# A graph network's aggregations on one core: gathering aligned chunks of edges and walking a list of (chunk, tile) pairs

## The chip, the cores and the metric

The kernel runs on one core of a Trainium2 chip. The metric is the device time of one execution in microseconds (us), from the first to the last instruction of that core; the number that counts is the median over several runs.

## What is computed

A graph has N = 6250 nodes with 256 features each (fp32) and E = 100000 edges `src -> dst`, sorted by `dst`. Four residual blocks follow one another. Each normalizes the node rows, and each contains one sum over the edges:

```
h = relu(layernorm(x));  x = x + block0(h): segment_sum(table0[src], dst), then experts
h = relu(layernorm(x));  x = x + block1(h): segment_sum(table1[src], dst)
h = relu(layernorm(x));  x = x + block2(h): segment_sum(table2[src], dst)
h = relu(layernorm(x));  x = x + block3(h): segment_sum(tensor_product(table3[src], edge weights), dst)
```

The edge weights of block 3 come from a small two-layer network on 8 numbers of every edge. The draw of `dst` is uneven: it is 6250 u² for a uniform u.

## The kernel before

**Tiles and windows.** The nodes lie in T = 50 tiles of P = 125 rows. `prepare` counts the edges of each tile and cuts each tile's edges into windows of 128 (`WIN`); a window belongs to one tile, so the last window of a tile is filled up with edges of the next one, which match no row of it. There are room and instructions for `WINDOWS` = 832 windows. The table `win_tab` holds each window's tile and first edge. Windows behind the last tile begin at edge E, where the padded edge list has `src` 0 and `dst` -1. `load_windows` gathers the windows' edges (8 indirect transfers of 104 windows) and turns them, so that `src_w[:, w]` and `dst_w[:, w]` are the 128 sources and local destinations of window w, in SBUF.

**One aggregation** (`aggregate`, run as agg0, agg1 and agg2 for blocks 0 to 2) makes 52 iterations of `WPI` = 16 windows, all written out:

- GpSimd (POOL) gathers the 128 rows of a window from the table in HBM into one of 16 buffers `msg` (L713), when VectorE has staged their indices (L726), which it does for four windows at a time once their buffers are free.
- VectorE (DVE) makes a one-hot matrix by comparing a row of numbers with `dst_w` (the match, L733), six windows ahead.
- TensorE (PE) multiplies one-hot and messages into one of four PSUM banks (L826, two passes of fp32), as soon as the gather has landed.
- VectorE adds the bank to the row block of the window's tile (L745; in agg0 also the in-degrees, L744). The tile comes out of a register: 16 of them are loaded at a time (`load_values`, L117).

Beside that, the same loop runs the edge network of block 3, in batches of 384 edges, two an iteration (262 batches: 104, 104 and 54): PE's L802 and L809, ScalarE's (ACT) L845, L854 and L855, and SyncE's (SP) loads of inputs (L887, L888) and stores of results (L893). agg0 and agg1 also do a product of the node's own rows in each iteration up to the 50th (L832, L834). In agg2 the one-hot matrices are stored (L898) for `tensor_product_edges`, the stage of block 3, which walks the same 832 windows and reads `src_w`.

**Counting.** In `prepare`, VectorE compares all destinations (125 x 800) with the upper bound of each of the 50 tiles, with a sum over the row (L375); PE adds over partitions, and a chain of small VectorE steps (`Chain`: each waits for the one before) makes the tables. After that VectorE makes the one-hot matrices of a histogram of `src` until the end of the stage.

Of the kernel before, what the change touches and what calls it, by code (L numbers as in the profile page):

```python
# [32 lines left out]
ds = bass.ds  # L33
# [10 lines left out]
STEPS = WINDOWS // WPI  # L44
BATCH = 3
# [14 lines left out]
assert N == P * T and E == P * EC and T % 2 == 0 and WINDOWS == WG * GROUPS_W and WG <= Q  # L60
assert EPAD >= E + WIN and 4 * STEPS < BATCHES <= 6 * STEPS and BATCHES % 2 == 0

# [52 lines left out]
def load_values(eng, row, most):  # L115

    return eng.bass.values_load_multi_w_load_instructions(  # L117
        row, engines=[eng.engine], min_val=0, max_val=most,
        skip_runtime_bounds_check_because="the table of windows is clamped to these bounds where it is written")[1]
# [24 lines left out]
class Net:  # L144


    def __init__(self, nc, ctx, a):
# [8 lines left out]
        self.src_w = sb("src_w", [Q, WINDOWS], I32)  # L156
        self.dst_w = sb("dst_w", [Q, WINDOWS])
        self.win_tab = sb("win_tab", [1, 2 * WINDOWS], I32)
# [104 lines left out]
def prepare(net, outb):  # L263
# [3 lines left out]
    with net.phase("prep") as ph:  # L267
# [7 lines left out]
        SCRATCH = 16  # L275
        scratch = [base[:, (9 + k) * EC:(10 + k) * EC] for k in range(SCRATCH)]
        tiles_bf, lanes_bf = ph.sb("tiles_bf", [P, EC], BF16), ph.sb("lanes_bf", [P, EC], BF16)
# [13 lines left out]
        past = ph.sb("past", [T, WINDOWS])  # L291
# [3 lines left out]
        iota_w = ph.sb("iota_w", [T, WINDOWS])  # L295
# [9 lines left out]
        with ph.block() as block:  # L305
            @block.gpsimd
            def _(pool):
# [10 lines left out]
                pool.wait_ge(s_const, 5)  # L318
# [33 lines left out]
            def _(act):  # L352
                act.wait_ge(s_ids[1], 96)
                for to, of, rows in ((net.edges, a["edge_index"], 192), (net.attr, a["edge_attr"], 192)):
# [3 lines left out]
                              a["edge_scal_t"].rearrange("k (r n) -> (k r) n", r=32)).then_inc(s_copies, 16)  # L358
                act.wait_ge(s_copies, 48)

            @block.vector
            def _(dve):
                step = Chain(dve, s_step)
                dve.memset(zero_bf[:, :], 0.0).then_inc(s_zero, 1)
                dve.wait_ge(s_const, 7)
                dve.tensor_copy(iota_bf[:, :], net.iota_i[0:P, 0:P])
                step(dve.tensor_scalar(bounds[:, :], net.iota_i[0:P, 0:T], float(P), float(P), ALU.mult, ALU.add))
# [3 lines left out]
                step(dve.tensor_copy(dst_f, ids[1]))  # L371
# [5 lines left out]
                dve.wait_ge(s_below, T)  # L377
                dve.tensor_copy(count[:, 0:1], below[:, 0:1])
                dve.tensor_tensor(count[:, 1:T], below[:, 1:T], below[:, 0:T - 1], ALU.subtract)
# [3 lines left out]
                dve.wait_ge(s_cnt, 2)  # L383
# [8 lines left out]
                dve.tensor_scalar(past[:, :], iota_w[:, :], col[:, 4:5], None, ALU.is_ge).then_inc(s_past, 1)  # L392
                dve.wait_ge(s_sum, 4 + 2 * GROUPS_W)
                for k in (0, 1):
# [11 lines left out]
                                  ALU.min, ALU.mult)  # L406
                dve.wait_ge(s_b2, 16)
                split_parts(Chain(dve, s_b2_split), dve, [part[:, :] for part in b2_parts], b2[:, :])

                dve.wait_ge(s_ids[0], 32)  # L410
# [16 lines left out]
            def _(pe):  # L427
                pe.wait_ge(s_const, 7)
                pe.wait_ge(s_below, T + 1)
                pe.matmul(small[0:T, 0:1], count[:, :], net.ones[0:P, 0:1], start=True, stop=True).then_inc(s_cnt, 1)  # L430
                pe.matmul(small[0:1, 2:3], bad[:, :], net.ones[0:P, 0:1], start=True, stop=True).then_inc(s_cnt, 1)
                pe.wait_ge(s_pairs, 1)
# [6 lines left out]
                for g in range(GROUPS_W):  # L439
# [3 lines left out]
                              start=True, stop=True).then_inc(s_sum, 1)  # L443
                pe.wait_ge(s_zero, 2)
# [137 lines left out]
def load_windows(net):  # L582

    with net.phase("windows") as ph:
        got = [ph.sb(f"got{g}", [WG, 2 * WIN], I32) for g in range(GROUPS_W)]
        src = [ph.sb(f"src{g}", [WG, WIN]) for g in range(GROUPS_W)]
        dst = [ph.sb(f"dst{g}", [WG, WIN]) for g in range(GROUPS_W)]
        s_got, s_flat, s_turned = ph.sem("got"), ph.sem("flat"), ph.sem("turned")
        of_src, of_dst = net.bank[0:2], net.bank[2:4]
        with ph.block() as block:  # L590
            @block.gpsimd
            def _(pool):

                for g in range(GROUPS_W):
                    pool.indirect_dma_start(
                        out=got[g][:, :], out_offset=None, in_=net.edges[:, :],
                        in_offset=bass.IndirectOffsetOnAxis(ap=net.first_edge[:, g:g + 1], axis=0)).then_inc(s_got, 16)

            @block.vector
            def _(dve):  # L600
                dve.wait_ge(s_got, 16 * GROUPS_W)
                for g in range(GROUPS_W):
                    dve.tensor_copy(src[g][:, :], got[g][:, 0::2]).then_inc(s_flat, 1)
                    dve.tensor_scalar(dst[g][:, :], got[g][:, 1::2], net.base_col[:, g:g + 1], None,
                                      ALU.subtract).then_inc(s_flat, 1)
                dve.wait_ge(s_turned, 2 * GROUPS_W)
                half = WINDOWS // 2
                for k in (0, 1):
                    dve.tensor_copy(net.src_w[:, k * half:(k + 1) * half], of_src[k][:, 0:half])
                    dve.tensor_copy(net.dst_w[:, k * half:(k + 1) * half], of_dst[k][:, 0:half])  # L610

            @block.tensor
            def _(pe):
                for g in range(GROUPS_W):
                    pe.wait_ge(s_flat, 2 * g + 2)
                    k, c = divmod(g, GROUPS_W // 2)
                    for of, to in ((src[g], of_src[k]), (dst[g], of_dst[k])):
                        pe.transpose(to[:, WG * c:WG * (c + 1)], of[:, :], net.ident[0:WG, 0:WG]).then_inc(s_turned, 1)
# [18 lines left out]
def aggregate(net, tag, table, degrees=False, root=None, shift=None, batches=(0, 0), kept_hots=None):  # L637
# [6 lines left out]
    GROUPS = 4  # L644
    PER = WPI // GROUPS
    AHEAD = 12
    HOTS, HOT_AHEAD = 8 if kept_hots is None else 16, 6
    KEPT = HOTS // BLOCK
    BANKS = 4
    with net.phase(tag) as ph:  # L650
        msg = [ph.sb(f"msg{r}", [Q, sums]) for r in range(WPI)]
        if kept_hots is None:
            hots = [ph.sb(f"hots{r}", [Q, BLOCK, HOT_W]) for r in range(KEPT)]
        else:
            size = BLOCK * HOT_W
            hots = [net.acc_full[:, T * D + r * size:T * D + (r + 1) * size].rearrange("p (b n) -> p b n", n=HOT_W)
                    for r in range(KEPT)]
        hot = [hots[r // BLOCK][:, r % BLOCK, :] for r in range(HOTS)]
        s_stored = [ph.sem(f"stored{r}") for r in range(KEPT)]
        idx = [ph.sb(f"idx{g}", [Q, PER], I32) for g in range(GROUPS)]  # L660
        s_idx, s_idle = ph.sem("idx"), ph.sem("idle")
        s_msg = [ph.sem(f"msg{r}") for r in range(WPI)]
# [31 lines left out]
        with ph.block() as block:  # L694
            @block.gpsimd
            def _(pool):
# [6 lines left out]
                if degrees:  # L703
                    for r in range(WPI):
                        pool.memset(msg[r][:, D:sums], 1.0).then_inc(s_ones, 1)

                def body(i, tile, last):
                    for g in range(GROUPS):
# [3 lines left out]
                        for r in range(PER):  # L712
                            pool.indirect_dma_start(  # L713
                                out=msg[PER * g + r][:, 0:D], out_offset=None, in_=table[:, :],
# [1264 lines left out]
```

## Time and profile before

| | us |
|---|---|
| median of 3 runs | 5958.91 (5951.58 to 5963.21) |
| the profiled execution, its own time | 5952.01 |
| its span (first to last instruction) | 5950.3 |

| engine | busy us (share) |
|---|---|
| PE matmul | 4674.6 (79%) |
| PE weight load | 3416.2 (57%) |
| DVE | 3725.1 (63%) |
| ACT | 1922.8 (32%) |
| POOL | 3687.2 (62%) |

The shares are means over stages that have different limits, so the views below are cut by stage. PE is TensorE's matmul, PEld its weight load, a "q" behind an engine's name its sequencer (register, semaphore and DMA-issuing work, not counted as busy). A row of the timeline is start, length, engine, line, operation, output <- inputs, count, and in brackets the idle time of the engine before it with what ended it. A row of the groups by line has busy time and mean ns of one, then idle time before it and what ended most of it. PEclk is the granted clock of TensorE as a share of full speed. A row of busy time by stage is the stretch (from:to), its length, the busy us (and count of instructions) of PE, PEld, DVE, ACT and POOL, then PEclk, the mean busy share of the DMA engines and GB/s.

### The profile page before, as it was taken

How to read it: one execution, taken by the hardware profiler on the slowest of the kernel's cores; microseconds unless marked ns; L12 is line 12 of the kernel's file. 1: busy time of each engine (PE TensorE's matmuls, PEld its weight loads, DVE VectorE, ACT ScalarE, POOL GpSimd, SP SyncE). 2: the span in 40 equal slices, each digit the busy share in tenths (PEclk: the TensorE clock that was granted, in tenths of full speed). 3: DMA queues.
4: the chain of work that ended last, by engine and by line, in shares of the span. 5: the costliest groups of instructions: out<-in, count | busy, mean ns of one | idle time of the engine just before them, and what ended most of it. 6: DMA issues, size and time to landing. Idle time of an engine off the chain costs nothing. (4 is left out here: it accounts for less than half of the span.)

```text
span 5950.3 us, 95247 instructions
## 1 busy us (share of the span) xinstructions
PE 4674.6 (79%) x22329; PEld 3416.2 (57%) x22329; DVE 3725.1 (63%) x11556; ACT 1922.8 (32%) x6042; POOL 3687.2 (62%) x4020
## 2 busy tenths in 40 slices
PE   3577777777499996777777767666777699999997
PEld 2554444445289995544444444433333588888887
DVE  8746666665812116655555554555555599999996
ACT  0142222222022222422222233221000577777774
POOL 0157777772066662477777746777777367777771
PEclk9999999996699998999999988999667699999998
DMA  6045555555099996455555556666555388888884
GB/s 176 16 130 148 147 146 148 148 148 98 1 338 338 339 336 171 117 148 146 147 148 148 148 98 176 198 199 195 157 157 157 71 248 260 259 261 259 259 260 99
DMA packets 694298, 1062.47 MB, mean 179 GB/s; under 512 B 212573, under 2 KB 534187, under 8 KB 693106
## 3 DMA queue, kind: packets, MB, share of 16 engines
q0 software_dynamic: 180864, 480.03, 30.6%
q1 hardware_dynamic: 512819, 571.84, 30.4%
q10 hardware_dynamic: 160, 5.63, 0.3%
q8 instruction: 151, 2.47, 0.2%
q14 instruction: 304, 2.49, 0.1%
HBM read 826.26 MB, written 236.47 MB: 179 GB/s over the span
## 5 line engine op out<-in xcount | busy, mean ns | idle before, releaser
L713 POOL DMA_INDIRECT agg_msg<-table,agg_idx x2496 | 2362.8, 947 | 760.3 <-issue 671.9
L745 DVE TENSOR_TENSOR acc<-acc,bank 125x256 f32 x2496 | 1051.3, 421 | 999.3 <-PE bank L826 948.0
L826 PE MATMUL bank<-agg_msg,agg_hots 128*125 128x257 f32 (+1 forms) x3328 | 1086.8, 421 | 530.0 <-DMA agg_msg<-table,agg_idx 337.0
L826 PEld LDWEIGHTS bank<-agg_msg,agg_hots 128*125 128x125 f32 x3328 | 545.6, 194 | 1061.5 <-DVE agg_hots L733 607.7
L1700 POOL DMA_INDIRECT tp_src<-table,tp_idx x832 | 807.0, 970 | 286.6 <-issue 252.4
L1714 ACT ACTIVATE tp_hots<-tp_hot,tp_weight 128x125 f32<-128x125 f32 x2496 | 814.2, 390 | 277.5 <-PE bank L1731 240.2
L826 PE MATMUL bank<-agg_msg,acc 128*125 128x256 f32 x1664 | 657.2, 502 | 291.5 <-DMA agg_msg<-table,agg_idx 209.8
L1731 PEld LDWEIGHTS bank<-tp_msg,tp_hots 128*125 128x125 f32 x4992 | 679.3, 189 | 47.4
L1731 PE MATMUL bank<-tp_msg,tp_hots 128*125 128x128 f32 x4992 | 684.1, 273 | 0.0
L826 PEld LDWEIGHTS bank<-agg_msg,acc 128*125 128x125 f32 x1664 | 312.8, 228 | 637.2 <-DVE acc L733 413.1
L854 ACT ACTIVATE agg_made<-bank,agg_made 128x128 f32<-128x128 f32 x786 | 288.6, 367 | 1174.2 <-PE bank L809 1162.3
L1727 PE MATMUL bank<-tp_msg,tp_hot 128*125 128x256 f32 x1664 | 557.9, 417 | 31.0 <-DVE tp_msg L1752 29.5
L1765 DVE TENSOR_TENSOR acc<-acc,bank 125x512 f32 x832 | 562.9, 677 | 2.3 <-issue 1.3
L733 DVE TENSOR_SCALAR agg_hots<-iota_i,dst_w 128x126 f32<-128x126 f32 x1664 | 503.9, 304 | 0.0
L809 PE MATMUL bank<-agg_fc,agg_hid 128*128 128x256 f32 x1572 | 486.7, 392 | 0.0
L1752 DVE TENSOR_TENSOR tp_msg<-tp_weight,tp_src 128x384 f32<-128x384 f32 x832 | 455.8, 548 | 0.0
L845 ACT ACTIVATE agg_hid<-bank 128x384 f32<-128x384 f32 x262 | 128.4, 490 | 805.9 <-PE bank L802 805.9
L1561 DVE COPY ffn_res<-bank 128x256 f32<-128x256 f32 x162 | 68.8, 425 | 503.9 <-DMA expert_rows<-ffn_res,moe_row_of_place 449.4
L744 DVE TENSOR_TENSOR deg_in<-deg_in,bank 125x1 f32 x832 | 129.5, 156 | 400.2 <-PE bank L826 380.6
L1474 POOL DMA_INDIRECT ffn_rows<-tokens,moe_token_of x162 | 158.0, 976 | 294.4 <-DVE ffn_b L1547 149.1
L809 PEld LDWEIGHTS bank<-agg_fc,agg_hid 128*128 128x128 f32 x1572 | 312.1, 199 | 48.8
L1537 ACT ACTIVATE ffn_hid<-bank,ffn_b 128x128 f32<-128x128 f32 x648 | 184.6, 368 | 440.4 <-PE bank L1513 440.4
(301 smaller groups left out, 6155.7 us busy)
## 6 DMA issues: line engine op xcount, KB each, us to landing
tp_weight<-edge_rows SPq DMA_DIRECT2D x832, 130.0 KB
edge_rows<-agg_made SPq DMA_DIRECT2D x262, 390.0 KB, 3.6
acc<-in_L_w_laid_dram SPq DMA_DIRECT2D x162, 512.0 KB
acc<-in_L_gnn_w_dram SPq DMA_DIRECT2D x162, 512.0 KB
kept_hots<-acc SPq DMA_DIRECT2D x208, 252.0 KB, 2.5
tp_hot<-kept_hots SPq DMA_DIRECT2D x208, 252.0 KB, 3.9
agg_msg<-table,agg_idx POOLq DMA_INDIRECT x2496, 3.0
table<-tab_out SPq DMA_DIRECT2D x40, 560.0 KB
```

The source lines that it names most:

```text
L713: pool.indirect_dma_start(out=msg[PER * g + r][:, 0:D], out_offset=None, in_=table[:, :], in_offset=bass.IndirectOffsetOnAxis(ap=idx[g][:, ...
L733: dve.tensor_scalar(hot[r % HOTS], net.iota_i[:, 0:HOT_W], net.dst_w[:, ds(WPI * i + r, 1)], None, ALU.is_equal).then_inc(s_hot, 1)
L745: dve.tensor_tensor(row, row, bank[0:P, 0:D], ALU.add).then_inc(s_add, 1)
L809: pe.matmul(wb[n % 2][:, 0:4 * MUL], hid[j % 2][:, c * Q:(c + 1) * Q], fc2[:, :, :].rearrange("p b n -> p (b n)"), start=True, stop=True). ...
L826: pe.matmul(net.bank[w % BANKS][0:P, 0:sums], hot[w % HOTS][:, 0:P], msg[w][:, :], start=True, stop=True).then_inc(s_sum, 1)
L854: act.activation(to[:, :, 0, :], of[:, :, 0, :], ACT.Copy, scale=made[j % 2][:, c, 4 * MUL:4 * MUL + 1])
L1700: pool.indirect_dma_start(out=src[w % R][:, :], out_offset=None, in_=table[:, :], in_offset=bass.IndirectOffsetOnAxis(ap=idx[w // WPI % 2] ...
L1714: ins = act.activation(hots[w % RM][:, c, :], hot[w // BLOCK % RB][:, w % BLOCK, 0:P], ACT.Copy, scale=weight[w % RW][:, 4 * MUL + 1 + c:4 ...
L1727: pe.matmul(out[:, 0:4, :], hot[w // BLOCK % RB][:, w % BLOCK, 0:P], m[:, 0:4, :], start=True, stop=False, skip_group_check=True)
L1731: mm = pe.matmul(out[:, 4 + c:8:3 - c, :], hots[w % RM][:, c, :], m[:, 4:6 + c:1 + c, :], start=False, stop=(c == 2), skip_group_check=True)
L1752: dve.tensor_tensor(quad, bc(wv[:, 2:4, :], 2, [Q, 2, 3, MUL]), bc(sv[:, 1:4, :], 1, [Q, 2, 3, MUL]), ALU.mult).then_inc(s_msg, 1)
L1765: dve.tensor_tensor(row, row, banks[w % len(banks)][0:P, :], ALU.add).then_inc(s_add, 1)
```

## The change

Aggregations no longer gather windows. The edge list is cut into 782 chunks of 128 consecutive edges whatever their tile, and each chunk is gathered once. A list of (chunk, tile) pairs, at most 782 + 49 = 831 and padded to 832, says which tile's rows a chunk is added to; PE, the match and the add make one step a pair. Which buffer of the ring of 16 a pair reads, and how many chunks must have landed, PE takes from registers, loaded 16 at a time from two new tables. SP waits for each gather in turn and counts it into one semaphore; it also waits until the pairs of four chunks are done (a third table) and tells POOL that four buffers are free. ACT now issues the loads and stores that SP issued. agg2 makes a second match a step, for the windows that block 3 still walks. `prepare` makes the pair list beside the window tables, and of the 50 counts 26 stay on VectorE while ScalarE makes 24 as sums of signs. `load_windows` gathers pairs and windows (16 transfers), loads the chunks with one, and stores `src_w` and `dst_w` to HBM; agg2 and `load_node_attr` load them back. The core of the diff:

```diff
+CHUNKS = -(-E // WIN)
+PAIRS = WINDOWS
+RING_C = 16
+PER_C = 4
```

In `prepare` (`BY_SIGN` is 26), on ScalarE and then on VectorE:

```diff
+                for b in range(BY_SIGN, T):
...
+                    act.activation(sign_scratch[n % SIGNS], dst_f, ACT.Sign, bias=middles[:, b:b + 1], scale=-1.0,
+                                   accum_out=signs[:, b:b + 1]).then_inc(s_sign, 1)
...
-                for b in range(T):
+                for b in range(BY_SIGN):
...
+                ceil_div(step, dve, tops[:, :], ends[:, :], WIN, twice_i[:, :], twice[:, :])
...
+                dve.tensor_scalar(past[:, :], iota_w[0:T, :], col[:, 5:6], None, ALU.is_ge).then_inc(s_pair_past, 1)
                 dve.wait_ge(s_b2, 16)
                 split_parts(Chain(dve, s_b2_split), dve, [part[:, :] for part in b2_parts], b2[:, :])
 
+                dve.wait_ge(s_pair_sum, 5 + 2 * GROUPS_W)
...
+                    dve.tensor_scalar(net.tile_of_pair[:, of], tile_h[k][TILE_ROW:TILE_ROW + 1, 0:HALF], float(T - 1), None,
+                                      ALU.min)
...
+                dve.tensor_scalar(net.landed_of_pair, chunk_row, 1.0, None, ALU.add)
```

In `load_windows`:

```diff
+                        out=got_p[g][:, :], out_offset=None, in_=net.edges[:, :],
...
+                        out=got_w[g][:, :], out_offset=None, in_=net.edges[:, :],
...
+                sp.dma_start(net.src_w[:, :], all_src[:, :]).then_inc(s_kept, 16)
+                sp.wait_ge(s_all, 4)
+                sp.dma_start(net.dst_w[:, :], all_dst[:, :]).then_inc(s_kept, 16)
```

In `aggregate`, first on POOL, then on DVE and PE:

```diff
-                        pool.wait_ge(s_idx, GROUPS * i + g + 1)
...
+                for c in range(CHUNKS):
+                    if c % PER_C == 0 and c >= RING_C:
+                        pool.wait_ge(s_free, (c - RING_C) // PER_C + 1)
                         carry_wait(pool, s_idle)
...
+                        in_offset=bass.IndirectOffsetOnAxis(ap=net.src_c[:, c:c + 1], axis=0),
+                    ).then_inc(s_msg[c % RING_C], 16)
...
-                        dve.tensor_copy(idx[r // PER][:, :].bitcast(F32),
...
+                            match(ahead)
+                            if kept_hots is not None:
+                                match_window(ahead)
...
+                    landed = load_values(pe, net.landed_of_pair[:, of], CHUNKS, least=1)
+                    slots = load_values(pe, net.slot_of_pair[:, of], RING_C - 1)
...
-                        pe.wait_ge(s_msg[w], 16 * i + 16)
-                        pe.matmul(net.bank[w % BANKS][0:P, 0:sums], hot[w % HOTS][:, 0:P], msg[w][:, :],
+                        pe.wait_ge(s_landed, landed[w] & COUNT_BITS)
+                        pe.matmul(net.bank[w % BANKS][0:P, 0:sums], hot[w % HOTS][:, 0:P], node_row(msg, slots[w]),
```

There on ACT, then on SP:

```diff
+                        if 1 <= j < count - 1:
+                            load(j + 1)
...
+                            store(j)
...
+                for c in range(CHUNKS):
+                    sp.wait_ge(s_msg[c % RING_C], 16 * (c // RING_C) + 16)
+                    sp.sem_inc(s_landed, 1)
+                    g = (c + 10) // PER_C
+                    if (c + 10) % PER_C == 0 and RING_C // PER_C <= g < GROUPS_C:
...
+                        sp.wait_ge(s_sum, gates[k % WPI] & COUNT_BITS)
+                        sp.sem_inc(s_free, 1)
```

In `load_node_attr`:

```diff
+                sp.dma_start(src_w[:, :], net.src_w[:, :]).then_inc(s_src, 16)
```

## Rows read from the trace of the kernel before

**Rows 1.** Busy time by stage: agg0, agg1, agg2, each with its tail.

```profile
349.60:1418.70 1069.10, 797.24 (x2796) 499.11 (x2796) 656.88 (x2698) 236.53 (x778) 787.44 (x832) 0.95 0.55 144
2453.80:3521.30 1067.50, 794.80 (x2796) 491.08 (x2796) 557.30 (x1915) 217.41 (x728) 786.91 (x832) 0.96 0.55 144
3601.50:4660.30 1058.80, 760.09 (x2100) 400.12 (x2100) 559.50 (x1916) 112.85 (x378) 788.34 (x832) 0.82 0.61 176
```

**Rows 2.** Groups by line, whole span: the gathers, two forms of ScalarE.

```profile
L713 POOL DMA_INDIRECT agg_msg<-table,agg_idx x2496 | 2362.8, 947 | 760.3 <-issue 671.9 <-DVE agg_idx L726 88.4
...
L1784 ACT ACTIVATE tab_rows<-x_res,nmr,rstd 125x256 f32<-125x256 f32 x150 | 90.4, 608 | 27.5 <-DVE nmr L1094 27.5
...
L1595 ACT ACTIVATE acc<-acc 125x256 f32<-125x256 f32 x50 | 17.6, 417 | 55.1 <-DVE acc L1627 55.1
```

**Rows 3.** Line L713, the gathers: length ns min/median/max, and landing.

```profile
L713 POOL DMA_INDIRECT agg_msg<-table,agg_idx x2496: 942/946/1013, 349.6 to 4642.1; - x192
...
DMA to landing us min/median/max: 2.6/3.0/15.9
```

**Rows 4.** Timeline at the end of agg0: the last gather, a late load.

```profile
1389.25 0.95 POOL L713 DMA_INDIRECT agg_msg<-table,agg_idx  x1 [0.30 <-issue]
...
1406.78 1.65 PE L802 MATMUL bank<-agg_scal,agg_fc 128*128 128x384 f32 x2 [10.49 <-DMA agg_made<-attr]
```

**Rows 5.** Timeline in agg2 while work is queued up on PE and DVE.

```profile
3612.51 0.42 DVE L745 TENSOR_TENSOR acc<-acc,bank 125x256 f32 x1
...
3612.84 0.28 DVE L733 TENSOR_SCALAR acc<-iota_i,dst_w 128x126 f32<-128x126 f32 x1
...
3613.14 0.42 DVE L745 TENSOR_TENSOR acc<-acc,bank 125x256 f32 x1
...
3614.37 1.27 PEld L826 LDWEIGHTS bank<-agg_msg,acc 128*125 128x125 f32 x6
...
3615.88 0.81 PE L802 MATMUL bank<-agg_scal,agg_fc 128*128 128x384 f32 x2
...
3616.53 0.38 PE L826 MATMUL bank<-agg_msg,acc 128*125 128x256 f32 x1
```

**Rows 6.** Instructions that read the window table: loads of 16 registers, ns.

```profile
L117 DVEq TENSOR_LOAD <-win_tab x208: 1095/1216/2349, 354.6 to 5830.0; - x104
L117 SPq TENSOR_LOAD <-win_tab x52: 967/977/1217, 4773.0 to 5811.7; - x52
```

**Rows 7.** Line L98, loop bookkeeping elsewhere: register work of TensorE's sequencer, ns.

```profile
L98 PEldq FUSED_REGOPS  x71: 44/44/50, 1428.2 to 5939.5; - x71
L98 PEldq ALU_OP  x71: 32/32/32, 1430.7 to 5941.6; - x71
```

**Rows 8.** Timeline of DVE in the counting and the tables.

```profile
8.75 1.05 DVE L375 TENSOR_SCALAR_CACHE_REDUCE acc<-acc,prep_bounds 125x800 f32<-125x800 f32 x1
...
9.72 1.04 DVE L375 TENSOR_SCALAR_CACHE_REDUCE acc<-acc,prep_bounds 125x800 f32<-125x800 f32 x1
...
60.98 0.15 DVE L235 TENSOR_SCALAR prep_col<-prep_col 50x1 f32<-50x1 f32 x1
61.16 0.15 DVE L236 TENSOR_TENSOR prep_col<-prep_col 50x1 f32<-50x1 f32 x1
...
74.17 0.58 DVE L396 TENSOR_SCALAR win_tab<-bank 1x416 int32<-1x416 f32 x1 [11.42 <-PE bank L442]
...
76.28 0.58 DVE L401 TENSOR_SCALAR win_tab<-acc 1x832 int32<-1x832 f32 x1
...
77.12 0.28 DVE L243 CAST prep_b_part<-prep_b 64x256 bf16<-64x256 f32 x1
...
78.97 0.58 DVE L250 CAST acc<-acc 125x800 f32<-125x800 int32 x1
```

**Rows 9.** Timeline of POOL in the window loads: the last of 8 gathers.

```profile
261.90 0.98 POOL L595 DMA_INDIRECT windows_got<-edges,first_edge  x1 [0.30 <-issue]
```

**Rows 10.** DMA issues: operation, KB each, median us from issue to landing.

```profile
edge_rows<-agg_made SPq DMA_DIRECT2D x262, 390.0 KB, 3.6
```

More of the change, by code:

```diff
@@ L406, in _ @@
                                   ALU.min, ALU.mult)
+                dve.tensor_copy(ends[:, 0:1], small[0:T, 3:4]).then_inc(s_pair, 1)
+                dve.tensor_scalar(some[:, :], col[:, 0:1], 0.0, None, ALU.is_gt).then_inc(s_pair, 1)
+                dve.wait_ge(s_pair, 2)
+                step(dve.tensor_tensor(ends[:, 1:2], ends[:, 0:1], col[:, 0:1], ALU.subtract))
+                ceil_div(step, dve, tops[:, :], ends[:, :], WIN, twice_i[:, :], twice[:, :])
+                step(dve.scalar_tensor_tensor(twice[:, :], tops[:, :], float(WIN), ends[:, :], ALU.mult, ALU.is_gt))
@@ L643, in aggregate @@
     acc = net.acc_view(D)
[L644 to L648, printed above, removed]
+    HOTS, HOT_AHEAD = 8, 6
+    KEPT = 4
     BANKS = 4
     with net.phase(tag) as ph:
[L651 to L662, printed above, removed]
+        msg = ph.sb("msg", [Q, RING_C, sums])
+        hot = [ph.sb(f"hot{r}", [Q, HOT_W]) for r in range(HOTS)]
+        if kept_hots is not None:
+            free, size = net.acc_full[:, T * D:2 * T * D], BLOCK * HOT_W
+            window_hots = [free[:, r * size:(r + 1) * size].rearrange("p (b n) -> p b n", n=HOT_W) for r in range(KEPT)]
+            dst_w = free[:, KEPT * size:KEPT * size + WINDOWS]
+            s_stored, s_dst, s_window = [ph.sem(f"stored{r}") for r in range(KEPT)], ph.sem("dst"), ph.sem("window")
+        s_idle, s_landed, s_free = ph.sem("idle"), ph.sem("landed"), ph.sem("free")
+        s_msg = [ph.sem(f"msg{r}") for r in range(RING_C)]
         s_hot, s_sum, s_add = ph.sem("hot"), ph.sem("sum"), ph.sem("add")
@@ L765, in body @@
                             dve.tensor_tensor(row, row, side[0:P, 0:D], ALU.add)
-                for r in range(0, AHEAD, PER):
-                    stage(0, r)
-                for r in range(HOT_AHEAD):
-                    match(0, r)
+                if kept_hots is not None:
+                    dve.wait_ge(s_dst, 16)
+                for p in range(HOT_AHEAD):
+                    match(p)
+                    if kept_hots is not None:
+                        match_window(p)
                 dve.sem_inc(s_add, BANKS)
@@ L865, in body @@
                             act.activation(node_root(net, i), side[0:P, 0:D], ACT.Copy).then_inc(s_rooted, 1)
+                act.wait_ge(s_empty, 5 if root or shift else 4)
+                load(0)
+                load(1)
                 iterations(act, body)
+                for b in (0, 1):
+                    act.wait_ge(s_kept[b], 16 * (count // 2))
+                if kept_hots is not None:
+                    for r in range(KEPT):
+                        act.wait_ge(s_stored[r], 16 * (WINDOWS // BLOCK // KEPT))
             @block.sync
```

313 lines of the change are left out of this document (208 added, 105 removed).

## Prediction

> **What bounds the kernel now.** I read the busy time by stage first. The three aggregations take 1069.1, 1067.5 and 1058.8 us [rows 1], together 3195.4, over half the span. PE, DVE and POOL all show idle time in them, so the shares don't name the limit. The second view, the groups by line, does: the 2496 gathers have 2362.8 us of work and 760.3 us of gaps in front of them, that is 3123.1 / 2496 = 1.251 us from one to the next, and 671.9 us of the gaps were ended by nothing but POOL's own issuing [rows 2]. The gap that is put down to VectorE's staged indices is no wait either: 0.30 us stands ahead of a gather with or without one. A gather's own length hardly varies, 942 to 1013 ns [rows 3]. So POOL issues gathers back to back, and 831 steps of 1.251 us are 1039.7 us of each stage: **the number of gathers sets the stage**, while PE and DVE follow.
>
> What is left of each stage is a tail behind the last gather: 1069.1 - 1039.7 = 29.4 us, then 27.8 and 19.1. A normal gather lands 3.0 us after its issue, the slowest after 15.9 [rows 3], and at the end of agg0 a small load of the edge network was also 10 us late [rows 4]. The place fits the padding. Counting the drawn `dst` by tiles of 125 nodes gives 808 windows with edges; the last 24 gathers fetch table row 0 on all 128 lanes. I read the tail as 24 gathers, and whatever shares the queues with them, crowding on one row.
>
> **The change part by part.** The sum starts from the profiled execution, 5952.0 us (span 5950.3); the median of the runs is 6.9 us above it, so 7 us of the answer are open by that alone.
>
> *Fewer gathers.* 782 chunks instead of 832 windows: 50 x 1.251 = 62.6 us a stage, **-187.7** for three. POOL's instructions stay the same (a wait and an increment ahead of every four). Four buffers come free when SP has seen the pairs of a group done; it looks when a chunk 10 ahead of POOL's next group has landed, so PE may lag 13 gathers (16 us) before POOL waits; a landing takes 3.0.
>
> *The tail.* Only the last chunk is padded, on 96 lanes. I expect landing 3, the crowded chunk 2, matmul and add 1, the last batch's copies and store 1 + 0.4 + 3.6 [rows 10], and 1 to leave: 12 us in agg0 and agg1, and 9 in agg2, which has no batch there. That is 17.4 + 15.8 + 10.1, **-43.3**. From below nothing of it comes (the tail has another cause); from above 51, if a tail is 8 us.
>
> *Does PE follow?* The list has 831 real pairs (same count of the inputs), so PE must do 832 steps in 977 us: 1.175 us a step, and 1.11 at the end, where tiles have 8 chunks and 9 pairs. Where work is queued, a pass of 256 columns takes 1.27 / 6 = 0.212 us and L802's two take 0.65 [rows 5]. Sixteen steps need 32 x 0.212 = 6.8, two batches 2 x (0.65 + 6 x 0.212) = 3.8, the node's own rows 6 x 0.212 = 1.3: 11.9, or 0.74 a step. New are two register loads in 16 steps. None is seen on PE; VectorE's take 1.22 (1.10 to 2.35), SP's 0.98 [rows 6]: 0.12 to 0.29 a step, I take 0.15. The address and the count to wait for are register work, 44 + 44 + 32 ns if it is like the loop bookkeeping [rows 7]: 0.12, or nothing where the sequencer runs ahead. Together 1.01, between 0.86 and 1.15: below 1.175, at its worst just over 1.11. Cost **0**. The cover is POOL's pitch; every 0.01 us above it would cost 8 us a stage. SP's relay of a landing is a wait and an increment, delay but no pitch.
>
> *Does DVE follow?* One add and one match take 3613.14 - 3612.51 = 0.63 us [rows 5]. agg2's second match makes it 0.91, and a register load in 16 steps 0.99 (1.06 if no two instructions overlap). That fits below 1.11. The staging copies (L726) go. Gathers average 5 ns above their minimum beside one match each [rows 2, 3]; a second match costs another 5 x 782, **+4**. agg2's first matches now wait for `dst_w`, about 5 us; POOL can issue 16 gathers (20 us) first, so it is hidden.
>
> *ACT's transfers.* ACT now waits for a batch's store (3.6 us [rows 10]) before it loads the next but has 8 steps, 9 us, for that and 2.5 us of own work; the load has some 3 steps left to land. **0**; if it is late, PE's in-order queue stalls at L802, and the ring of 16 takes up to 16 us of it.
>
> *Counts and tables.* 24 comparisons of 0.97 us leave VectorE [rows 8]: -23.3. ScalarE does 24 beside its 26 (25.2 us, and 2 for the order test). One of 800 columns is not seen: 256 columns take 0.42 to 0.61 [rows 2], so 1.30 to 1.90 in proportion and less by their fixed share. I take 1.1, 26.4 and a table load, just hidden: +0.5; at 1.90 it is +20. The pair list repeats the window list on the same path: 19 chained steps of 0.18 = 3.4, a hop to PE and a comparison 1.3, PE's second set of products 11.4 (the wait in front of L396), four half rows at 0.5, eight whole rows at some 0.75 (a half row's 0.58 is the bound below, twice it above), 0.9 of small ones; the splitting from L243 to L250, 1.85, now runs inside that wait. Together 3.4 + 1.3 + 11.4 + 2 + 6 + 0.9 - 1.85 = 23.2. Net **+1**, between -8 and +22.
>
> *Loading windows.* Eight more gathers at 0.98 + 0.30 [rows 9] are 10.3, and behind them the store of the two tables, like the 390 KB store 3.6 + 0.4 [rows 10]. All of it is alone on the path: **+14.3** (10 to 20). Reading one back in `load_node_attr`: **+1.5** (0 to 4).
>
> Sum: 5952.0 - 187.7 - 43.3 + 4 + 1 + 14.3 + 1.5 = **5742**.
>
> **A rule against it.** The gathers keep their length of 942 to 1013 ns although a match runs beside most of them [rows 3], and that row is what I go by. The Trainium skill (SBUF — State Buffer, Who interferes with whom) says that a VectorE `tensor_scalar` in its two-port mode locks GpSimd out of their shared ports for the whole instruction, and that descriptors can't be written meanwhile. By that rule 832 more matches stall agg2's gathers; that is the rival "locked gathers" below.
>
> **The rivals.**
> *PE becomes the bound* (the one on the other side). Place: the register loads and waits ahead of each pair in PE's queue. For it: nothing in this trace shows PE loading registers or waiting for a register's value. Against it: 1.01 of 1.175. At 1.20 us a step each stage takes 832 x 1.20 + 14 = 1012 instead of 989: 5811. It decides when three stages take what they did less the 17 us added elsewhere, (3195.4 - 17) / 3 = 1059, (1059 - 14) / 832 = 1.256 us a step; above that the kernel is slower, at 1.30 by 92 + 17: 6061.
> *agg2 alone is bound*, by its second match or by PE at the half clock: without batches, in the last half, two passes at 1.2 GHz are 0.86 by the rate above, and 0.27 of loads and registers make 1.13 (agg2's granted clock is 0.82 [rows 1]). At 1.20 on all its steps +23: 5765.
> *Locked gathers.* 832 x 0.28 us = 233 in agg2: 5742 - 4 + 233 = 5971, slower. Against it: the spread of 71 ns.
> *ScalarE is slow at counting*, 1.90: +20, 5762.
> *The tail stays.* If the last gathers were late for another reason than their common row, -43 is lost: 5785. Late landings only there speak against it.
>
> **How the numbers follow.** Chances: the forecast 0.68, agg2 bound 0.10, ScalarE slow 0.08, the tail stays 0.05, PE at 1.175 to 1.256 0.04, PE above that 0.03, locked gathers 0.02. The likeliest gives 5742, by itself 5718 (short tails, a cheap list, no stretch: -24) to 5760 (the run's 7 and a dearer list). The range for 8 in 10 takes in the cases at 5762, 5765 and 5785 and leaves out bound PE and locked gathers: **5712 to 5800**. A change under 0.2% (12 us) is about what a measurement of this kernel can't tell from none. Faster 0.94, same 0.01, slower 0.05, the last from the two cases that lie above.
>
> **What would show it.** 782 gathers a stage still 1.25 us apart, with all gaps ended by issue: right. Gaps ended by a wait for SP's count, or gathers longer than 1 us in agg2: PE, DVE or the ports. PE's register loads over 2 us, or a step that never falls under 1.2 us when messages lie ready: PE. The stages should last near 989, 989 and 990 us. The wait of VectorE for ScalarE's signs should be short, and the histogram should start where it did, at 79 us. The window stage should be 14 us longer. The prediction fails if PE's steps follow its own register work rather than POOL.

## The result, and the profile after

The changed kernel takes 5733.52 us (median of 4 runs, 5724.15 to 5739.86), 0.9626 of the time before (95% interval 0.9614 to 0.9637). The forecast was 5742, its range 5712 to 5800. The profiled execution took 5734.1 us with a span of 5732.1, 218.2 less than before.

Busy time by stage, agg0, agg1, agg2 with their tails, as in [rows 1]:

```profile
363.40:1350.90 987.50, 762.24 (x2796) 549.44 (x2796) 641.52 (x2493) 238.52 (x779) 740.31 (x782) 0.91 0.55 149
2383.70:3372.00 988.30, 768.53 (x2796) 552.14 (x2796) 546.65 (x1710) 219.21 (x729) 740.63 (x782) 0.91 0.55 149
3452.00:4442.00 990.00, 683.81 (x2100) 437.26 (x2100) 679.59 (x2549) 113.74 (x379) 743.98 (x782) 0.84 0.61 182
```

The stages were forecast at 989, 989 and 990. Together they are 2965.8 us against 3195.4 in [rows 1]: -229.6, and so all of the gain and a little more lies in them. The gathers again, one stage each by line (they answer to [rows 2]), and their lengths and landings over all stages (to [rows 3]):

```profile
L847 POOL DMA_INDIRECT agg_msg<-table,src_c x782 | 740.3, 947 | 238.1 <-issue 232.9 <-SPq L1057 5.2
L847 POOL DMA_INDIRECT agg_msg<-table,src_c x782 | 740.6, 947 | 238.1 <-issue 234.8 <-SPq L1057 3.4
L847 POOL DMA_INDIRECT agg_msg<-table,src_c x782 | 744.0, 951 | 238.1 <-issue 227.4 <-SPq L1057 10.7
```

```profile
L847 POOL DMA_INDIRECT agg_msg<-table,src_c x2346: 942/946/1091, 363.4 to 4432.9; - x196
...
DMA to landing us min/median/max: 2.7/2.9/5.4
```

(740.3 + 238.1) / 782 = 1.251 us from one gather to the next, as before. The gaps put down to SP's release of buffers (L1057) are ordinary ones of 0.30 us; the idle time is 238.1 in each stage, so POOL waited for nothing. The slowest landing fell from 15.9 us to 5.4. In agg2 a gather is 4 ns longer.

The end of agg0, as in [rows 4]: the last gather, the last add, the first instruction of the next stage, and from the view by line the drains of the engines' sequencers (ns, start):

```profile
1340.69 0.95 POOL L847 DMA_INDIRECT agg_msg<-table,src_c  x1 [0.30 <-issue]
...
1345.85 0.42 DVE L873 TENSOR_TENSOR acc<-acc,bank 125x256 f32 x1
1350.96 1.28 ACT L2052 ACT_TABLE_LOAD   x1 [6.89 <-PEq L225]
```

```profile
L831 POOLq DRAIN  x1: 18699/18699/18699, 1330.8 to 1330.8; - x1
...
L831 DVEq DRAIN  x1: 434/434/434, 1345.9 to 1345.9; - x1
...
L831 ACTq DRAIN  x1: 14/14/14, 1347.1 to 1347.1; - x1
```

The sum is done at 1346.3 and ACT, with its last store, at 1347.1. But POOL's drain began at 1330.8 while gathers were still queued and lasted 18.7 us, to 1349.5. That is 7.90 us behind the end of the last gather (1340.69 + 0.95 = 1341.64), and it ends the stage. It is 7.90 in agg1 and agg2 too.

PE's and the others' loads of registers, as in [rows 6], in the three stages, and PE's register work, as in [rows 7], ns:

```profile
L128 PEldq TENSOR_LOAD <-tables x312: 1099/1194/2637, 368.7 to 4420.4; - x156
L128 DVEq TENSOR_LOAD <-tables x156: 1095/1599/2637, 368.6 to 4420.2; - x156
L128 SPq TENSOR_LOAD <-tables x36: 967/973/1754, 373.8 to 4346.8; - x36
```

```profile
L955 PEldq FUSED_REGOPS  x2496: 46/46/52, 371.4 to 4436.6; - x192
...
L954 PEldq ALU_OP  x2496: 32/32/36, 371.3 to 4436.5; - x192
```

DVE in the counting and the tables (to [rows 8]), then ScalarE's signs, ns:

```profile
9.16 1.04 DVE L425 TENSOR_SCALAR_CACHE_REDUCE acc<-acc,prep_bounds 125x800 f32<-125x800 f32 x1
...
36.22 0.17 DVE L430 TENSOR_SCALAR below<-prep_signs 125x24 f32<-125x24 f32 x1
...
51.72 0.58 DVE L448 TENSOR_SCALAR tables<-bank 1x416 int32<-1x416 f32 x1 [11.42 <-PE bank L532]
...
54.66 0.14 DVE L459 COPY prep_ends<-bank 50x1 f32<-50x1 f32 x1
...
70.90 0.36 DVE L480 CAST tables<-bank 1x192 int32<-1x192 f32 x1 [9.29 <-PE bank L545]
...
79.94 0.57 DVE L270 CAST acc<-acc 125x800 f32<-125x800 int32 x1
```

```profile
L404 ACT ACTIVATE acc<-acc,prep_middles x24: 944/945/962, 9.6 to 31.3; 125x800 f32<-125x800 f32 x24
```

DVE did not wait for the signs: the last one began at 31.3 and DVE used them at 36.2. The pair list costs 79.94 - 54.66 = 25.3 us where the window list ended before. The work behind it starts at 79.94, against 78.97 in [rows 8].

The window stage (to [rows 9]): its last gather, the two stores, and the first load of the next stage:

```profile
273.14 0.98 POOL L709 DMA_INDIRECT windows_got_w<-edges,first_edge  x1 [0.30 <-issue]
...
279.75 0.35 SPq L718 DMA_DIRECT2D src_w<-acc  x1
280.75 0.33 SPq L720 DMA_DIRECT2D dst_w<-acc  x1
286.01 0.40 SPq L1354 DMA_DIRECT2D tab_w<-in_L_gnn_W_gc_dram  x1
```

### The profile page after: what moved, and what is told of

It is laid out like the page before. It is cut to its first block and busy times, and to the rows that moved or that the text cites. A ratio compares the mean times of both kernels' runs of the same rounds, so it can differ in the third digit from the quotient of the medians.

```text
span 5732.1 us, 104292 instructions
## 1 busy us (share of the span) xinstructions
PE 4555.9 (79%) x22391; PEld 3581.1 (62%) x22391; DVE 3810.9 (66%) x11775; ACT 1948.3 (34%) x6091; POOL 3555.5 (62%) x3880
## 3 DMA queue, kind: packets, MB, share of 16 engines
q1 hardware_dynamic: 270449, 411.16, 22.6%
## 5 line engine op out<-in xcount | busy, mean ns | idle before, releaser
L847 POOL DMA_INDIRECT agg_msg<-table,src_c x2346 | 2224.9, 948 | 714.2 <-issue 695.1
L955 PE MATMUL bank<-agg_msg,agg_hot 128*125 x4992 | 1663.8, 445 | 736.8 <-SPq L1050 510.5
L955 PEld LDWEIGHTS bank<-agg_msg,agg_hot 128*125 128x125 f32 x4992 | 990.2, 214 | 1317.3 <-issue 1163.6
L855 DVE TENSOR_SCALAR agg_hot<-iota_i,dst_p 128x126 f32<-128x126 f32 x2496 | 774.0, 311 | 53.0 <-PEq L1110 29.2
L1654 PE MATMUL bank<-ffn_cols,acc 128*128 128x128 f32 x2592 | 318.8, 276 | 6.7 <-DVE ffn_cols L1695 2.6
L1868 PEld LDWEIGHTS bank<-tp_msg,tp_hot 128*125 128x125 f32 x1664 | 245.5, 186 | 120.1 <-issue 38.1
## 6 DMA issues: line engine op xcount, KB each, us to landing
kept_hots<-acc ACTq DMA_DIRECT2D x208, 252.0 KB, 2.9
tp_hot<-kept_hots SPq DMA_DIRECT2D x208, 252.0 KB
```

Of the source, the lines that this page charges most:

```text
L847: pool.indirect_dma_start(out=msg[:, c % RING_C, 0:D], out_offset=None, in_=table[:, :], in_offset=bass.IndirectOffsetOnAxis(ap=net.src_c[ ...
L855: dve.tensor_scalar(hot[p % HOTS][:, :], net.iota_i[:, 0:HOT_W], net.dst_p[:, p:p + 1], None, ALU.is_equal).then_inc(s_hot, 1)
L955: pe.matmul(net.bank[w % BANKS][0:P, 0:sums], hot[w % HOTS][:, 0:P], node_row(msg, slots[w]), start=True, stop=True).then_inc(s_sum, 1)
L1654: mm = pe.matmul(hidden[b % 2][:, j * Q:(j + 1) * Q], w1[b % R][:, c, j * Q:(j + 1) * Q], cols[b % 2][:, c, :], start=(c == 0), stop=(c == ...
L1868: pe.matmul(out[:, 0:4, :], hot[w // BLOCK % RB][:, w % BLOCK, 0:P], m[:, 0:4, :], start=True, stop=False, skip_group_check=True)
```

## The experiments

Each run's expectation is quoted as it was put on record. The kernel before, run beside each group of them, took from 5948.6 to 5960.2 us (medians, in two groups a single run), so a difference of some 10 us between two medians says little by itself; lengths of stages and gathers are read from the traces. The theory throughout: POOL's gathers, 1.251 us apart, set the three stages; a tail made by gathers that crowd on row 0 stands behind them; the tables and the window stage stand alone on the path. The main rivals: other engines' steps share the bound, and the tail has another cause.

### Fewer gathers alone (before_skip50)

```diff
+                            if PER * g + r == WPI - 1 and 1 <= i <= 50:
+                                continue
                             pool.indirect_dma_start(
...
```

> The kernel before without the gathers of 50 windows in each aggregation (window 15 of iterations 1 to 50; the sum uses the rows that lie in the buffer), nothing else changed: no pair list, no registers, no relay. Theory (POOL's gathers set the stage): 3 x 50 x 1.251 = -187.7, 5764 us, with the tails as before. Rival 1 (PE's and VectorE's 832 steps set it too): less than half of that, above 5858. Rival 2 (the changed kernel's gain comes in part from its longer run ahead or from ACT's transfers, not from the number of gathers): -120 to -170 here.

Measured: 5771.47 us (5763.72 to 5776.52), 0.9694 of before [0.9678, 0.9711]. The stages:

```profile
349.70:1357.40 1007.70, 767.57 (x2796) 487.25 (x2796) 648.97 (x2699) 237.30 (x779) 740.88 (x782) 0.97 0.57 146
2391.20:3396.70 1005.50, 770.14 (x2796) 491.02 (x2796) 554.15 (x1917) 218.09 (x728) 740.06 (x782) 0.97 0.57 146
3475.70:4472.00 996.30, 707.16 (x2100) 403.82 (x2100) 555.47 (x1916) 113.20 (x378) 740.43 (x782) 0.85 0.64 180
```

3195.4 - 3009.5 = 185.9 us for 150 gathers, 1.24 each, with no walk of pairs, no relay and the old code on ACT and SP. For the three stages the number of gathers is the cause; both rivals fall. The profiled execution as a whole is only 179.2 us shorter (5950.3 - 5771.1): block 3, which this run does not touch, took 8.0 us longer from its first gather to its last.

### The tail: padding that reads different rows (before_spread), and row 0 put back (after_crowd)

```diff
-    edge_index[E:, 0] = 0
+    edge_index[E:, 0] = np.arange(0, 10 * (EPAD - E), 10)
```

> The kernel before, but the padded edges behind edge E carry 608 different sources instead of 0, so that the last 24 windows gather distinct rows. Theory (the tail behind the last gather is those 24 gathers crowding on one row): the tails fall from 29.4, 27.8 and 19.1 us to what the changed kernel shows, 10.2, 10.6 and 9.0: -46.5. Block 3 walks the same windows, and in the changed kernel its POOL still waits 14.4 and 4.0 us once each among the last 24 gathers: another -15 to -19. Together 5952 - 46.5 - 17 = 5889 us in the profiled execution. Rival (the last gathers are late because the stage ends, or for other traffic): 5952, tails as before.

```diff
...
+                dve.memset(net.src_c[:, CHUNKS - 24:WC * LOADS_C], 0)
```

> The changed kernel, with the source list of its last 24 chunks set to row 0 (those edges' true rows are left out of the sums). Theory (crowding on one row makes the tail): the tails go from 10.2, 10.6 and 9.0 us back to about 29, 28 and 19, together +46, 5780 us. Rival (the tail came from the windows' walk or from SP's stores of the edge network): no change, 5734.

Measured: before_spread 5880.0 us (5879.76 to 5888.63), 0.9884 [0.9867, 0.99]; after_crowd 5785.05 (5783.1 to 5788.68), 51.5 above the changed kernel. First the stages and the landings of before_spread, then the stages of after_crowd:

```profile
349.50:1395.30 1045.80, 785.20 (x2796) 488.00 (x2796) 656.64 (x2698) 237.26 (x778) 787.32 (x832) 0.97 0.54 147
2431.90:3478.00 1046.10, 788.33 (x2796) 484.30 (x2796) 557.00 (x1916) 218.06 (x728) 787.07 (x832) 0.97 0.54 147
3559.10:4604.30 1045.20, 751.38 (x2100) 404.89 (x2100) 559.09 (x1917) 113.23 (x378) 787.81 (x832) 0.83 0.60 178
```

```profile
DMA to landing us min/median/max: 2.6/2.8/5.5
```

```profile
361.90:1367.10 1005.20, 772.75 (x2796) 560.17 (x2796) 638.31 (x2497) 238.45 (x779) 740.67 (x782) 0.90 0.56 147
2410.30:3415.60 1005.30, 770.03 (x2796) 559.26 (x2796) 545.16 (x1710) 219.10 (x729) 740.74 (x782) 0.90 0.56 147
3494.80:4496.00 1001.20, 699.82 (x2100) 441.26 (x2100) 680.51 (x2549) 113.32 (x379) 743.55 (x782) 0.82 0.63 180
```

One constant in the inputs takes 3195.4 - 3137.1 = 58.3 us out of the old kernel's stages, and row 0 on 24 chunks puts 3011.7 - 2965.8 = 45.9 into the new one's (46 expected), where the slowest landing is 15.4 us again. That the tail comes from the last 24 gathers all reading one row is shown from both sides; only row 0 was tried. One part of before_spread's expectation missed: block 3 was to lose 15 to 19 us between its gathers and lost 5.4 (1064.2 to 1058.7 from first to last); the time behind its last gather fell by 11.3 as well. The old kernel with spread padding even leaves its stages sooner than the changed kernel, 5 to 7 us behind the start of the last gather instead of 9 to 10.7; the drain below is why.

### Spread padding in the changed kernel (after_spread)

The same line is changed.

> The changed kernel with 608 different sources on the padded edges. In the changed kernel POOL's drain ends each aggregation, 7.90 us behind the end of the last gather in all three; in the kernel before with spread padding it ended 3.98 behind. Theory (the 96 padded lanes of the last chunk still crowd on row 0, and so do the 24 padded windows of block 3): 3 x 3.9 = -11.8, and block 3 loses its waits of 14.4 and 4.0 and about 4 us of late landings, -17 to -20: together -29 to -32, 5703 us. Rival (the drain takes 7.9 us because of the chunk walk, for instance the deeper run ahead of 16 gathers): only block 3 gains, 5715.

Measured: 5722.77 us (5708.36 to 5725.31), 10.7 below the changed kernel, where 29 to 32 were expected. The drain did not move (agg0's ends at 1332.0 + 17.6 = 1349.6, 7.90 behind its last gather), so the 96 padded lanes are not what it waits for. That is the rival's outcome, only block 3 gains; its reason, the chunk walk, is not shown by it. In the changed kernel its last padded windows hold POOL up twice:

```profile
5607.85 0.94 POOL L1841 DMA_INDIRECT tp_src<-table,tp_idx  x1 [3.06 <-DVE tp_msg L1893]
...
5626.12 0.94 POOL L1841 DMA_INDIRECT tp_src<-table,tp_idx  x1 [13.49 <-DVE tp_msg L1893]
```

With spread padding no two gathers there start more than 1.6 us apart, and first to last gather of that stage falls from 1073.7 us to 1059.1.

### What the drain is (after_ends, early_columns)

```diff
+                for c in range(CHUNKS + 2 if tag == "agg0" else CHUNKS):
...
+                        if tag != "agg1":
+                            carry_wait(pool, s_idle)
...
+                if tag == "agg2":
...
+                    pool.wait_ge(s_msg[c % RING_C], 16 * (c // RING_C) + 16)
...
```

> The changed kernel with a different end of POOL's program in each aggregation, to see what its drain waits for (7.90 us behind the end of the last gather in the changed kernel, 3.98 in the kernel before with spread padding). agg0: two further gathers of padding behind the last, 784 in 196 whole groups of four; agg1: no increment of the idle semaphore ahead of each group; agg2: POOL waits for the last chunk's landing before it drains. Theory (the drain is longer behind a group of two than behind one of four): agg0's falls to about 4.0 behind its last gather, the others stay at 7.9. Rival 1 (the increments): only agg1's falls. Rival 2 (a fixed time behind the last gather, whatever stands between): all three 7.9.

Measured (one run): 5734.27 us, the drains 8.07, 7.90 and 10.49 us behind the end of the last gather. agg2's is the telling one, since POOL had waited for its last gather's landing before it drained:

```profile
L831 POOLq DRAIN  x1: 7900/7900/7900, 4434.2 to 4434.2; - x1
```

With every gather landed, the drain takes 7.90 us by itself. So those 7.90 are no wait for the gathers, and none of the three theories has it right: groups and increments change next to nothing, and the time counts from POOL's last instruction, here the wait. In before_spread it is 3.98 (1378.1 + 15.84, behind a gather that ended at 1389.92). Neither figure holds everywhere. Where the last 24 gathers read row 0, the drain ends 16.7 to 17.7 us behind the last gather in the kernel before and 19.0 to 19.5 in after_crowd, so slow transfers do hold it. And in block 3 of before_spread and after_spread, a stage of 832 gathers, it ends 2.6 and 2.5 us behind the last one. One guess was the number of index columns, 16 staged ones before and 782 now:

```diff
+                turn = {"agg0": 16, "agg1": 128, "agg2": CHUNKS}[tag]
...
-                        in_offset=bass.IndirectOffsetOnAxis(ap=net.src_c[:, c:c + 1], axis=0),
+                        in_offset=bass.IndirectOffsetOnAxis(ap=net.src_c[:, c % turn:c % turn + 1], axis=0),
```

> The kernel with the early gathers (5693 us), in which agg0 takes its gathers' rows from the first 16 columns of the source table over and over, agg1 from the first 128, agg2 from all 782 as before (agg0's and agg1's sums are then those of other rows). POOL's drain at the end of a stage takes 7.90 us by itself, and 3.98 in the kernel before, where the indices came from 16 staged columns. Theory (the drain grows with the number of index columns read since the last one): about 4.0 in agg0, between 4.0 and 7.9 in agg1, 7.9 in agg2; 3.9 us fewer in agg0. Rival (it grows with the form of the loop or of the buffers): 7.9 in all three.

Measured (one run): 5702.07 us, 7.91, 7.90 and 7.90: not the columns. What doubles the drain, some 4 us in each of three stages, stays open.

### How near PE is (after_loads, after_loads2)

```diff
+                    for _ in range({"agg0": 8, "agg1": 2, "agg2": 0}[tag]):
+                        load_values(pe, net.tile_of_pair[:, of], T - 1)
```

> The changed kernel with further register loads on PE, 16 registers each, ahead of every 16 steps: 8 more in agg0, 2 more in agg1, none in agg2. Theory (the loads stand in PE's step, 0.074 us a step each, beside 0.74 + 0.12): agg1's step is 0.86 + 4 x 0.074 = 1.16, just below POOL's 1.175, so agg1 stays at 988 (up to +10); agg0's is 0.86 + 10 x 0.074 = 1.60, 832 x 1.60 + 14 = 1345, +358: together about 6095. Rival 1 (PE's sequencer runs ahead of the array and hides them): both stages stay at 988, 5734. Rival 2 (a load holds PE up for more than its own time): agg1 above 1020.

Measured: 5735.64 us (5727.81 to 5745.05), no change, but it tells nothing: the trace has 104 loads on PE in agg0, as in the changed kernel. The added loads, whose values nothing uses, are not in the program that ran. The second try reloads the two rows that are used:

```diff
+                        if w in {"agg0": (0, 3, 6, 10, 13), "agg1": (0, 8), "agg2": (0,)}[tag]:
+                            landed = load_values(pe, net.landed_of_pair[:, of], CHUNKS, least=1)
+                            slots = load_values(pe, net.slot_of_pair[:, of], RING_C - 1)
```

> The changed kernel, in which PE loads the same two rows of registers again between the steps of an iteration, so that each load's values are used: 10 loads in 16 steps in agg0 (ahead of steps 0, 3, 6, 10, 13), 4 in agg1 (0, 8), 2 in agg2 as in the changed kernel. Theory (each load stands in PE's step with some 1.2 us): agg1's step 0.86 + 4 x 0.075 = 1.16, 988 us (up to +10); agg0's 0.86 + 10 x 0.075 = 1.61, 1350 us, +362, together about 6097. Rival 1 (the loads lie beside matmuls that are queued already, and are hidden): both at 988, 5734. Rival 2 (a load also waits until PE has finished, and costs more): agg1 above 1020, agg0 above 1400.

Measured (one run): 5755.94 us. The stages agg0 and agg1, the loads in agg0, and its gathers by line:

```profile
362.10:1373.20 1011.10, 702.60 (x2796) 509.24 (x2796) 636.13 (x2493) 237.90 (x779) 740.33 (x782) 0.99 0.53 146
2411.10:3400.10 989.00, 760.82 (x2796) 557.58 (x2796) 541.65 (x1710) 218.68 (x729) 740.65 (x782) 0.91 0.54 149
```

```profile
L128 PEldq TENSOR_LOAD <-tables x520: 1099/1106/1963, 367.5 to 1365.6; - x174
```

```profile
L847 POOL DMA_INDIRECT agg_msg<-table,src_c x782 | 740.4, 947 | 252.0 <-issue 224.6 <-SPq L1058 27.4
```

PE's matmuls of step 416 in agg0 (counted from 0), and those of its last two steps, 830 and 831:

```profile
873.82 0.69 PE L956 MATMUL bank<-agg_msg,agg_hot 128*125 x2 [1.84 <-DVE agg_hot L855]
...
1368.21 1.03 PE L956 MATMUL bank<-agg_msg,agg_hot 128*125 x4
```

Ten loads of 1.1 us in 16 steps make PE the bound in the second half of the stage. From step 416 to 830 a step takes (1368.21 - 873.82) / 414 = 1.194 us, where the changed kernel's PE, following POOL, takes (1344.13 - 872.83) / 414 = 1.138. The loads are the only edit, though the wait that ends last in front of a matmul is now often one for DVE's match, which itself follows PE. PE falls behind, and from 1123.7 on POOL waits for SP's release: its idle time rises from 238.1 to 252.0, and the time behind the last gather from 10.2 to 19.8. But the stage is 23.6 us longer, not 362: 1.194 us a step, where the sum of terms gave 1.61. With four loads (agg1) the stage is 0.7 us longer. The loads lie largely beside matmuls that are queued already. One thing helped PE here: the granted clock of agg0 was 0.99, in the changed kernel 0.91, and its matmuls took 762.2 - 702.6 = 59.6 us less, 0.07 a step. At the lower clock the same loads could cost up to that much more (an estimate from these rows).

### A second match beside the gathers (after_match)

```diff
+                                dve.tensor_scalar(spare[ahead % 2][:, :], net.iota_i[:, 0:HOT_W], net.dst_p[:, ahead:ahead + 1],
+                                                  None, ALU.is_equal)
```

> The changed kernel with one more match a step in agg0 and agg1, into spare buffers that nothing reads; agg2 has its second match already. Theory (a match beside a gather stretches it by some ns, as agg2's pitch of 1.2560 beside agg1's 1.2518 shows): agg1 +3.3, pitch 1.256, DVE's step 0.99. In agg0 DVE also adds the degrees, step 1.14 to 1.21 against 1.175 of POOL: +3 to +33. Together 5740 to 5770. Rival 1 (a match holds POOL up for its whole 0.28 us): +219 in each, 6170. Rival 2 (agg2's longer pitch comes from its stores of 252 KB): agg1 unchanged, 988.

Measured: 5748.18 us (5743.87 to 5753.97), with the gathers of agg0 and agg1:

```profile
L848 POOL DMA_INDIRECT agg_msg<-table,src_c x782 | 743.4, 951 | 238.1 <-issue 230.2 <-SPq L1061 7.9
L848 POOL DMA_INDIRECT agg_msg<-table,src_c x782 | 743.0, 950 | 238.1 <-issue 231.4 <-SPq L1061 6.7
```

A gather is 3 to 4 ns longer (947 before), 3.1 and 2.4 us a stage, where agg2's were 3.7 above agg0's; most of agg2's excess needs no stores, and DVE is no bound in agg0 either. The other 9 us of the median are not in these stages and are not explained; the profiled execution's span lay 12.1 above the changed kernel's, 6 of it behind block 3's last gather, where executions differ.

### All counts on VectorE (after_counts)

```diff
-        BY_SIGN = 26
+        BY_SIGN = 49
```

> The changed kernel with 49 of the 50 counts on VectorE and one on ScalarE. Theory (the counts lie on the path to the tables, 0.967 us each): 23 x 0.967 = +22.2, 5756 us, and the histogram starts at 102 us instead of 80. Rival (the stage ends with something else, such as the clearing stores or the product of PE, so that the start of the histogram costs nothing): 5734.

Measured: 5756.38 us (5755.49 to 5758.87), 22.9 above the changed kernel. The work behind the tables starts 102.18 - 79.94 = 22.2 us later:

```profile
102.18 0.57 DVE L270 CAST acc<-acc 125x800 f32<-125x800 int32 x1
```

### A faster version: the window gathers in the shadow of the histogram (after_early)

POOL does nothing while `prepare` makes its histogram, and the tables are ready before that. Spread padding is in it too.

```diff
+                pool.wait_ge(s_copies, 48)
+                pool.wait_ge(s_first, 2)
+                net.gather_windows(pool, s_got)
+                pool.wait_ge(s_got, 16 * 2 * GROUPS_W)
...
```

> The changed kernel with spread padding, and the 16 window and pair gathers and the chunk load issued in prepare as soon as their tables lie ready (POOL is idle there during the histogram); load_windows only turns them, windows first, so that their stores run beside the rest. Theory (the gathers stood alone on the path): the window stage falls from 31 us to about 12, -19 to -21 against the same kernel with spread padding alone: 5683. Rival (the gathers slow the histogram by VectorE's share of the ports, or the stores now end the stage): -5 to -12, 5692 to 5698.

Measured: 5692.81 us (5689.81 to 5701.55), 0.9558 of the kernel before [0.9545, 0.9571], 40.7 below the changed kernel and 30.0 below after_spread. DVE from the end of the histogram, the first and last copies of the window stage, the next stage; then the gathers, ns:

```profile
250.62 0.21 DVE L538 TENSOR_SCALAR deg_out<-bank 125x50 f32<-125x50 f32 x1 [1.24 <-PE bank L583]
253.00 1.18 DVE L741 CAST windows_src_w<-acc 104x128 f32<-104x128 int32 x8 [2.16 <-PEq L617]
...
261.25 1.08 DVE L761 COPY dst_p<-bank 128x416 f32<-128x416 f32 x2
262.63 0.19 DVE L2054 TENSOR_SCALAR root_out<-deg_out 125x50 f32<-125x50 f32 x1 [0.30 <-PEq L729]
```

```profile
L217 POOL DMA_INDIRECT acc<-edges,first_edge x8: 984/1270/1745, 81.0 to 92.1; - x8
L217 POOL DMA_INDIRECT acc<-edges,first_edge_p x8: 1282/1290/1300, 93.7 to 104.8; - x8
```

The histogram ends when it did (250.6, against 250.4 in the changed kernel), the window stage takes 10 us instead of 33, and the first gather of agg0 comes at 340.5 instead of 363.1 in after_spread: 22.6 us. By block 3 it is 19.7; the other 11 lie in the closing stage behind block 3's last gather, which took 95.0 us here and 106.2 there. That is not explained: the closing stage took 99.1 to 111.2 us in after_counts, the changed kernel and after_loads, which are the same in it.

## Why the prediction was right

*What bounds.* Right. The stages came out at 987.5, 988.3 and 990.0, and before_skip50 shows the slope of 1.24 us a gather without anything else of the change.

*Fewer gathers, and agg2's match.* First to last gather of the three stages is 2935.9 us against 3119.4: -183.5, where -187.7 + 4 = -183.7 was forecast. after_match shows most of the 4 to be the second match. *Locked gathers* falls with it: the longest gather in agg2 is 1091 ns. The Trainium skill (SBUF — State Buffer, Who interferes with whom) asks for a two-port mode if a `tensor_scalar` is to lock GpSimd out; nothing in these runs shows a match to be in one. Two rows of agg2 speak against a fast mode, since 126 columns of a match, compared with a column of `dst_w`, take longer than 192 columns that are multiplied by a constant:

```profile
3461.67 0.27 DVE L861 TENSOR_SCALAR acc<-iota_i,acc 128x126 f32<-128x126 f32 x1
3461.86 0.25 DVE L901 TENSOR_SCALAR agg_fc<-agg_fc 128x192 f32<-128x192 f32 x1
```

What a VectorE instruction in such a mode does to a gather is not shown here.

*The tail.* Right in cause and nearly in size, the size in part by luck: 10.2, 10.7 and 9.1 us where 12, 12 and 9 were forecast, -46.2 instead of -43.3. The steps given for what is left (landing, matmul and add, the last batch's copies and store) are not what ends it. In agg0 they are over 6.4 us behind the start of the last gather, half of the 12; POOL's drain, which the forecast did not have, ends the stage 7.90 behind that gather's end and makes up for most of the rest. The 2 us for the crowded last chunk are not borne out: with its rows spread (after_spread) the drain ends where it did. Against the old kernel with spread padding, the change loses 4 us a stage there.

*PE.* Cost 0, right: the matmuls of the last step start 4.0 to 4.4 us behind the start of the last gather. The terms were too dear. Loads, waits and register work were added to the matmuls as if nothing ran beside them (1.01 a step); ten loads where two were should then have given 1.61 and gave 1.194, at a higher granted clock. The longest load, 2.6 us, was over the 2 that the text allowed, and costs nothing.

*DVE, and ACT's transfers.* 0, right. PE has no idle time in front of the edge network's first product (L928) in any stage, so no load was late. The wait for `dst_w` at the start of agg2 was taken for about 5 us and is longer: the first match stands at 3459.43, 7.5 us behind the first gather, where in agg1 it stands 2.0 ahead of it. The ring of 16 hides it all the same: POOL's gathers go on 0.30 us apart, and from first to last they take 3.3 us more than agg1's, which their own length accounts for.

*Counts and tables.* +1 forecast, 0.97 measured: a sign takes 0.945 from one to the next (1.1 assumed), and the pair list takes 25.3 instead of 23.2 + 1.85. after_counts measures the signs' share by itself, 22.2.

*Loading windows.* +12.8 (13.8 at agg0's first gather, less 0.97), where 14.3 was forecast; reading back +0.82 (3.81 us from the first instruction of that stage to the next stage's, 2.99 before) instead of 1.5.

The terms sum to -215.0; another 3.2 us fell in stages that the change does not touch. So the forecast lay 8 us above the profiled execution: 2.9 of it in the tails, 2.2 in the window stage and the read back, the rest in those stages.

## What to carry to other kernels

Where one engine issues back to back and its gaps are ended by its own issuing, count its instructions: here 150 gathers fewer were worth 1.24 us each, and the new bookkeeping on four engines cost nothing in those stages. Look at what padding reads: 24 gathers of 128 lanes on one row are 3% of a stage's gathers and cost a tail in every stage that walked them, while the 96 padded lanes of a single chunk made no difference to its stage; one constant took 58 us out of the old kernel's stages. And ask of each new step on the path whether its engine was idle earlier with the inputs ready: the window gathers, moved 170 us ahead into POOL's idle time, gave back some 20 us.

## What had not been expected of the hardware

- POOL's drain at the end of an aggregation ends 7.90 us behind the last gather in the changed kernel and 3.98 in the old one with spread padding, the same in all three stages of each; behind gathers that crowd on one row it ends 17 to 20 us behind. What sets the 7.90 and the 3.98 is open.
- Gathers beside the histogram take 1.29 us (0.98 in the window stage, [rows 9]) and fall into step with VectorE, whose compares of two bf16 operands take 1.20 and 0.57 us and come back every 1.60; 1.29 + 0.30 is 1.59. Gathers beside a match keep their 0.95. The Trainium skill (SBUF — State Buffer, Who interferes with whom) says that a VectorE instruction with two SBUF inputs contends with a GpSimd instruction that reads SBUF; a gather reads its indices there, and these rows agree; no run takes the two apart, so the cause is argued.
- With ten register loads in 16 steps, agg0's mean granted clock of TensorE was 0.99 of 2.4 GHz instead of 0.91, and its matmuls' busy time fell from 762.2 to 702.6 us. In the changed kernel the clock set none of the three stages: agg2 ran at 0.84, and its gathers were still 0.30 us apart.
